# First stage's edge-key fetches in 14 blocks of unequal sizes in place of 12 of 128 rows and one of 32

## The reference

```python
h = jnp.maximum(_layernorm(x, axis=-1), 0.0)
hn = _layer_norm(h, ln1_w, ln1_b)
ft = (hn @ W_att).reshape(n, H, DH)          # written to a table, gathered by edge later
...
m = jax.ops.segment_max(scores, dst, num_segments=n)
out = jax.ops.segment_sum(msg, d, num_segments=n_nodes)   # as a product with an adjacency matrix
```

## Time and profile before

| | us |
|---|---|
| time before, median of 3 runs | 3986.43 |
| lowest and highest of the 3 | 3984.04, 3987.22 |
| span of the profiled execution | 3987.6 |
| first stage, start of the span to the first instruction behind the barrier | 116.43 |
| POOL's 1568 gathers of the attention stage, busy and idle between them | 1483.0 + 478.0 |
| PE busy over the span | 3679.6 (92%) |
| DVE, ACT, POOL busy over the span | 2167.3, 1880.8, 1505.2 |

### The profile page before, as it was taken

One profiled execution on the slowest core, in us unless ns is written; L12 is line 12 of the kernel. 1 busy time (PEld: TensorE's weight loads), 2 busy tenths in 40 slices (PEclk: granted clock), 3 DMA queues, 4 the chain that ended last, 5 costly groups with the idle time before them and its releaser, 6 DMA issues. The chain is left out here.

```text
span 3987.6 us, 61840 instructions
## 1 busy us (share of the span) xinstructions
PE 3679.6 (92%) x21902; PEld 2157.9 (54%) x21902; DVE 2167.3 (54%) x3396; ACT 1880.8 (47%) x5147; POOL 1505.2 (38%) x1605
## 2 busy tenths in 40 slices
PE   5899999999999999999985879999999999999999
PEld 3566666666666666666653544445444544454444
DVE  8788888888888888888874750002100210012000
ACT  4788888888888888888863660002000100011000
POOL 2677777777777777777760000000000000000000
PEclk8788888888888888888886989999999999999999
DMA  6443333333333333333334126665666566665665
GB/s 202 128 109 104 105 106 105 105 106 105 106 105 105 106 106 106 105 106 105 105 92 88 38 65 204 204 196 181 199 194 208 174 194 203 205 189 184 213 204 159
DMA packets 467250, 560.45 MB, mean 141 GB/s; under 512 B 45449, under 2 KB 411684, under 8 KB 466686
## 3 DMA queue, kind: packets, MB, share of 16 engines
q1 hardware_dynamic: 383558, 366.63, 30.4%
q0 software_dynamic: 51168, 107.68, 12.2%
q10 hardware_dynamic: 32248, 82.62, 5.6%
HBM read 455.16 MB, written 103.20 MB: 140 GB/s over the span
## 5 line engine op out<-in xcount | busy, mean ns | idle before, releaser
L900 POOL DMA_INDIRECT fts<-ft_tab,src_all x1568 | 1483.0, 946 | 478.0 <-issue 477.4
L2171 PE MATMUL cv_acc<-cv_cnt,cv_parts 128*128 128x512 bf16 (+1 forms) x7056 | 1431.3, 366 | 0.0
L2171 PEld LDWEIGHTS cv_acc<-cv_cnt,cv_parts 128*128 128x128 bf16 x7056 | 666.0, 98 | 761.7
L2006 DVE TENSOR_TENSOR cv_y<-cv_acc,dis_row 128x512 f32<-128x512 f32 (+1 forms) x52 | 34.4, 661 | 1355.1 <-PE cv_acc L2171 1326.5
L937 DVE TENSOR_TENSOR ohk<-iota_ps,key_cols 128x784 bf16<-128x784 f32 x784 | 724.9, 966 | 6.1
L1030 ACT ACTIVATE dist_l<-lo_iota,low 128x128 bf16<-128x128 f16 x1960 | 593.7, 388 | 18.6 <-ACT low L1025 0.8
L1189 PE MATMUL agg_ps<-terms,oh 128*64 128x141 f32 x2744 | 528.7, 364 | 25.6 <-DVE terms L974 25.0
L1189 PEld LDWEIGHTS agg_ps<-terms,oh 128*64 128x64 f32 x2744 | 458.1, 180 | 80.6 <-DVE terms L974 67.3
L1082 ACT CAST strip<-adj_ps 128x392 bf16<-128x392 f32 x784 | 372.2, 475 | 271.4 <-PE adj_ps L1133 239.2
L1133 PE MATMUL adj_ps<-ohk,ohl 128*128 128x196 bf16 x3136 | 431.2, 263 | 0.0
L951 DVE TENSOR_TENSOR prod<-ftd_ps,fts 128x780 f32<-128x780 f32 (+1 forms) x392 | 271.1, 692 | 220.5 <-DMA fts<-ft_tab,src_all 212.3
(11 more groups left out here) (261 smaller groups left out, 2919.9 us busy)
## 6 DMA issues: line engine op xcount, KB each, us to landing
cv_cnt<-adj SPq DMA_DIRECT2D x96, 2048.0 KB, 8.3
cv_cnt<-adj SPq DMA_DIRECT2D x48, 2176.0 KB, 8.6
adj<-strip ACTq DMA_DIRECT2D x196, 392.0 KB
fts<-ft_tab,src_all POOLq DMA_INDIRECT x1568
win<-ft_tab SPq DMA_DIRECT2D x196, 65.0 KB
agg_tab<-res SPq DMA_DIRECT2D x196, 35.2 KB
cv_cnt<-adj SPq DMA_DIRECT2D x8, 512.0 KB, 3.7
agg_tab<-zero_f SPq DMA_DIRECT2D x10, 352.5 KB
```

The source lines that it names most:

```text
L900: nc.gpsimd.indirect_dma_start(fts[u][:, k, :], None, ft_tab[:, :], bass.IndirectOffsetOnAxis(src_all[:, n, k:k + 1], 0)).then_inc(gathere ...
L2171: last = nc.tensor.matmul(a[:, 0:width], parts[:, r, b, :], cnt[q][:, 0:width // SUB, (b - b0) * SUB:(b - b0 + 1) * SUB], start=(b == 0 an ...
```

## The change

The blocks get sizes from a table: 128, 127, 126, 125, 124, 122, 121, 120, 119, 112, 96, 64, 63 and 121 rows, 1568 together as before. There are 14, where there were 13. `FETCH_AT` holds where each begins. All loops over blocks run to 14; `pair` puts block 12 (63 rows) and block 13 (121 rows) into cycle 7, which before had the block of 32 alone. `fetch_places` issues one DVE instruction per block. The destinations of the two copies are the same addresses in another notation.

```diff
-BLOCKS = -(-NH // P)
+FETCH = (128, 127, 126, 125, 124, 122, 121, 120, 119, 112, 96, 64, 63, 121)
+BLOCKS = len(FETCH)
+FETCH_AT = tuple(sum(FETCH[:b]) for b in range(BLOCKS))
...
-        in_block = lambda b: min(P, NH - b * P)
+        in_block = lambda b: FETCH[b]
...
-            pool.wait_ge(s["start_at_made"], 2)
+            pool.wait_ge(s["start_at_made"], BLOCKS)
...
-                nc.vector.scalar_tensor_tensor(to, turned_keys, -float(KSTEP * P * b),
+                nc.vector.scalar_tensor_tensor(to, turned_keys, -float(KSTEP * FETCH_AT[b]),
...
-                nc.vector.tensor_scalar(start_at[:, 0:BLOCKS - 1], cnt_ps[:, 0:BLOCKS - 1], 2.0 * COARSE, None, ALU.mult
-                                        ).then_inc(s["start_at_made"], 1)
-                nc.vector.tensor_scalar(start_at[0:NH % P, BLOCKS - 1:], cnt_ps[0:NH % P, BLOCKS - 1:BLOCKS], 2.0 * COARSE,
-                                        None, ALU.mult).then_inc(s["start_at_made"], 1)
+                for b in range(BLOCKS):
+                    m = in_block(b)
+                    nc.vector.tensor_scalar(start_at[0:m, b:b + 1], cnt_ps[0:m, b:b + 1], 2.0 * COARSE, None, ALU.mult
+                                            ).then_inc(s["start_at_made"], 1)
...
-                last = nc.tensor.matmul(cnt_ps[0:m, b:b + 1], start_f[0:1, b * P:b * P + m], ones[0:1, 0:1],
+                last = nc.tensor.matmul(cnt_ps[0:m, b:b + 1], start_f[0:1, FETCH_AT[b]:FETCH_AT[b] + m], ones[0:1, 0:1],
                                         start=True, stop=True)
```

More of the change, by code:

```diff
@@ L430, in key_columns @@
                 m = in_block(b)
-                to = key_cols[:, b * P // NA:(b * P + m) // NA].rearrange("p g a c -> p c (g a)")
+                to = key_cols[:].rearrange("p g a c -> p (g a) c")[:, FETCH_AT[b]:FETCH_AT[b] + m, :].rearrange("p s c -> p c s")
                 turned_keys = block_ps[b % 2][:, 0:SC * m].rearrange("p (c n) -> p c n", c=SC)
                 dve.wait_ge(s["keys_turned"], b + 1)
-                nc.vector.scalar_tensor_tensor(to, turned_keys, -float(KSTEP * P * b),
+                nc.vector.scalar_tensor_tensor(to, turned_keys, -float(KSTEP * FETCH_AT[b]),
                                                strip_no[:, 0:m].unsqueeze(1).to_broadcast([P, SC, m]), ALU.add, ALU.subtract
@@ L635, in low_columns @@
                 m = in_block(b)
-                to = low_cols[:, b * P // NA:(b * P + m) // NA].rearrange("p g a c -> p c (g a)")
+                to = low_cols[:].rearrange("p g a c -> p (g a) c")[:, FETCH_AT[b]:FETCH_AT[b] + m, :].rearrange("p s c -> p c s")
                 act.wait_ge(s["key_cols_made"], b + 1)
```

## The result

The changed kernel takes 3997.8 us, median of 8 runs (3996.29 to 4001.69), against 3985.56 of before in the same comparison (8 runs, 3983.14 to 3989.26). The ratio is 1.0032, with a 95% interval of 1.0022 to 1.0041: 12 us slower, between 9 and 16. Forecast were 9.3 us, 3995.7, in a range of 3986.5 to 3999.

What follows compares the result with a forecast made beforehand. POOL's gathers bound the attention stage, so only the first stage's end counts: 8.5 (block 1) + 0.9 (cycle 7) - 0.1 (shorter blocks) = +9.3 us, giving 3995.7 us, range 3986.5 to 3999.

Steps and rivals of the forecast that it cites:

- The first stage's end is the kernel's end: Attention stage stays 1961 us of POOL's gathers, so each microsecond the first stage ends later lengthens the kernel by one.
- Engines by divisor: Uneven fetches: the largest number up to 16 dividing the rows gives the DMA engines, one for 127; chance 0.50.
- Block 1's landing: Cycle 1: 127 rows on one engine land at 68.8 instead of 58.5, DVE's copy 8.5 us later (7.7 to 11.5).
- Fetch places: DVE's two place instructions become 14, adding 0.9 us, hidden inside the wait for block 1.
- The other blocks: Later uneven fetches land before use; tightest is block 5, landing at 78.3 and wanted by PE at 82.2.
- Cycle 7: Last cycle of the first stage: PE's second block adds 0.6, ACT's copies 0.3, together 0.9 us (0.9 to 1.4).
- The -0.1: Blocks used up to cycle 7's end are 88 rows shorter in total, saving 0.1 us.
- The even spread: Rival: every fetch deals its rows to all 16 engines, no wait for block 1; +1.7 us, 3988.1, chance 0.38.
- the one engine for each uneven block: Rival: no divisor but 16 counts, block 5 lands 1.3 behind PE; +10.6 us, 3997.0, chance 0.07.
- The point from which block 1's wait costs nothing: Cycle 1: block 1 landing by about 61.2 costs nothing, reached from three engines.

Runs made afterwards that it cites:

- the 13 even blocks: Changed kernel with 12 blocks of 128 rows and one of 32, one place instruction each; 3987.32 us beside 3984.78 for the kernel before.
- the run with the 127 rows alone: Changed kernel with 13 blocks: block 1 of 127 rows, the last of 33, all others 128; 3994.47 us, ratio 1.0023 against the kernel before.

## Why the prediction was right

The mechanism was the forecast one, step by step:

- *The first stage's end is the kernel's end.* POOL hardly waits in the attention stage in any run: of the 478 us between its gathers at most 0.9 is anything but "issue". The stage grew by 10.4, the time by 12.2 (9 to 16). The 1.8 between them lies within the interval, and cannot be told from the scatter of the gathers' 3.7 us.
- *Engines by divisor.* Right, and now shown on the queue and for the kind of copy where the trace of before had nothing: 127 rows on one engine (busy share 0.07, one late step of the semaphore), 122 on two and 123 on three (two and three late steps). The Trainium skill (DMA: Bandwidth & Descriptors, "Why a DMA increments its semaphore by 16 and not by 1") has the divisor rule, and the exception that would have spread some direct copies from GpSimd; these indirect fetches follow the rule, and the exception was not met.
- *Block 1's landing.* Forecast 13.9 after its issue, 15.1 came. POOL's own work was 1.62 more than an even fetch takes, the upper end that the rows had given (1.6), of which I took half: 0.8 of the miss. The transfer took 11.3, not 10.5. Its rate in the quiet stretch was as forecast, 25 GB/s against 24.8, but one of its first packets took 0.8 where most take 0.16. What is left of the landing, 2.2, was less than the 2.6 put down for it. With all this DVE's copy came 9.7 later, not 8.5. This is the term that was mis-sized, inside the 7.7 to 11.5 kept for it.
- *Fetch places.* 0.92 from the first to the next work, where two took 0.15: 0.77 more, 0.9 forecast. They were covered in the changed kernel, as said, and came into the open where block 1 landed in time (0.65 in the 13 even blocks).
- *The other blocks.* Blocks 2 to 4 landed at 69.2, 71.1 and 71.3 and were used from 71.2 on; block 5 landed at 79.7 and was used at 82.0. All had cover, block 5 with 2.3 where I had 3.9.
- *Cycle 7.* 0.6 between the same two rows, 0.9 forecast. PE's second block put the product 0.4 later, not 0.6, and ACT's longer and second copy 0.2, not 0.3. The landing of the last write and the barrier took 0.2 more.
- *Sum:* 9.7 + 0.6 + 0.2 - 0.1 = 10.4, 9.3 forecast. The -0.1 is what is left for the cycles between the two places. That it equals the forecast for shorter blocks is luck as much as anything, for the same cycles took 0.8 longer in the run with the 127 rows alone.

The even spread is refuted by the landings, the one engine for each uneven block by 122 and 123 rows. The point from which block 1's wait costs nothing was put at three engines; the later landing of an uneven fetch moves it beyond. Four or more engines were not run in that place.

## What to carry to other kernels

The rows of an indirect fetch are a choice with a cliff. Here 128 rows land in 3.6 us and 127 in 15, and rounding them up to a multiple of 16 gave the 8 us of the stage back, though rows were fetched that nobody uses. Whether such a fetch costs anything is decided by the distance between its issue and its use, so a fetch that has to be uneven belongs where that distance is long: the same 127 rows cost nothing that can be told as block 10. And a stage ahead of one that is bound by a single engine is worth its full length, however idle everything looks in it.

## What the runs showed of the hardware

POOL's work for an indirect fetch grows with the rows on the busiest engine: 0.95 with 8, 1.43 with 41, 1.69 with 61 and 2.57 to 2.58 with 127, all on 0.014 us a row. The rows of the fetch do not matter for it, 128 cost less than 122.

A slow fetch holds up the landing of all that are issued behind it, though fifteen engines are free. In the changed kernel block 2, on fourteen engines, landed 0.2 behind block 1 and 12.4 after its own issue. Where block 10 was the slow one, blocks 11 to 13 landed 0.4 to 1.6 behind it, after waits of up to 13.5. The data can be there long before. Of block 2's 16 semaphore steps 15 had come by 61.2, and the last came at 69.15; on the engine that was still busy with block 1 the trace has only packets of 4 and 8 bytes for block 2, behind the last row of block 1. Block 3 had a share of its rows there, which moved from 68.5 to 70.6.

The fetches bring small packets with them when they are uneven. The pages of before and after, in this order:

```profile
DMA packets 467250, 560.45 MB, mean 141 GB/s; under 512 B 45449, under 2 KB 411684, under 8 KB 466686
```

```profile
DMA packets 469218, 560.47 MB, mean 140 GB/s; under 512 B 47377, under 2 KB 413612, under 8 KB 468654
```

There are 1928 more packets under 512 bytes, and one fetch more explains 16 of them. 1832 have 8 bytes, and the fetches of before have none of these. They are not what makes the landing of the 127 rows late. In the run with 127 rows alone 945 of them, 15 times 63, pass between 57.99 and 59.83, ten microseconds before the landing. In the changed kernel the engine that carries the rows has none of them between its own packets. Whether they slow its first packets stays open; no run here took them away alone.
